# Plain columns of a split-precision matmul kernel: 96 wide in two matmuls per k, or 128 wide in three

## The chip, the cores and the metric

The kernel runs on one core of a Trainium2 chip. The metric is the device time of one execution in microseconds, the median of several runs. The profile comes from one execution, recorded by the hardware profiler.

## What is computed

Eight sequences of 256 tokens with 1024 features go through an adapter matrix chosen by an id for each sequence, then through a base layer with a routed low-rank (LoRA) part, and are added to the input:

```python
y      = einsum('bsi,boi->bso', x, weight[ids])            # stage 1, 1024 x 1024 per sequence
base   = einsum('btd,od->bto', y, base_W) + base_b         # stage 2
logits = einsum('btd,nd->btn', y, router_W) + router_b     # 15 router outputs
probs  = softmax(logits); topk_p, topk_i = top_k(probs, 8)
w      = einsum('btk,btke->bte', topk_p, onehot(expert_map[topk_i]))
h      = einsum('btd,erd->bter', y, A)                     # 8 experts x rank 16
out    = x + base + einsum('bter,eor->bto', h * w[..., None], B) * 2.0
```

## The kernel before

Everything is float32. Each operand of a matmul is split into a high part in the float32r format and a low part (value minus high part), and a product a x b is three matmuls: hi x hi, hi x lo, lo x hi. ScalarE writes the high parts (copies with a cast), VectorE the low parts (subtractions). Each matmul is preceded by its own load of 128 x 128 weights.

An **element** is one of the eight sequences (b). It has two stages on TensorE.

Stage 1 (`stage1_chunk`, L825 and L827) makes y in eight chunks of 128 outputs, eight steps of k each: one matmul of 512 columns (w_hi against x_hi and x_lo side by side) and one of 256 (w_lo against x_hi). ScalarE and VectorE add the two halves into y_sum and split it into y_hi and y_lo, and form differences of blocks of y (`sums`, `sums_lo`, `fourth`).

Stage 2 multiplies y by base_W, the router and A. Its 1024 output columns are divided in three: N1 and N2, NH = (1024 - NP)/2 wide, and PLAIN, NP wide between them. N1 and N2 are done by a block scheme with 7 instead of 8 half products (`product`, L860 to L862: 4 steps of k, three matmuls of NH columns each; 7 calls an element, 8 plain calls in element 0). The block combinations of base_W are in `st_hi` and `st_lo`. The three widths hang together: NP = 96 gives NH = 464.

The plain part (`plain`, L850 and L851) holds what is multiplied by the ordinary rule: AR = 8 x 16 + 15 + 1 = 144 columns for A, the router and one column of padding, and the NP plain columns of base_W; PL = AR + NP = 240. `pl_split[:, k, 0, :]` is the high part, `pl_split[:, k, 1, :]` the low part, and they lie side by side. For each of two token tiles t and eight k, L850 multiplies y_hi by both (2 x PL = 480 columns) and L851 adds y_lo times the high part to the first 240 columns. The product y_hi x lo thus stands in a second half of columns of `pl_ps`, and other engines add the halves: for the routing, ScalarE copies the second half (`ar_part`, L411) and VectorE adds the first (L581, in `routing_logits`); for the plain output columns, VectorE adds both halves to res in two instructions (`add_plain`, L641 and L643).

The order on TensorE in stage 2 of an element (`stage2`): plain, product into x_ps, into z_ps (from the differences S1), into x_ps (S2), the transposes of the gated h (L881), product into w_ps, x_ps, z_ps, three groups of three LoRA matmuls of 512 columns (`lora_b`, L875 to L877), one more product and one more LoRA group. Between them stand waits for the other engines by semaphores: s_lo_done (VectorE L557) before the z_ps product, hw_done (the end of the routing chain, L618) before the transposes, s4_lo_done (L570) before the last z_ps product, hwt_lo_done (L625) before the LoRA matmuls, x_added and z_added (VectorE's additions into res, L633 and L636) before the reuse of their tiles. Element 0 has its own order (`first_stage2`), in which the blocks of base_W are still being split (L699). Elements 1 to 6 run in a loop, element 7 stands behind it. SyncE issues nearly all transfers, GpSimd those with addition.

Of the kernel before, what the change touches and what calls it, by code (L numbers as in the profile page):

```python
# [12 lines left out]
ALU = mybir.AluOpType  # L13
# [23 lines left out]
def adaln_ffn_kernel(nc, xT, x, ids, wT, a_t, base_t, b_t, router_t, base_b, router_b, expert_map, out):  # L37
    NB, _, KC, T = xT.shape
    OC = wT.shape[1]
    D = KC * P  # L40
    NT = T // P
# [4 lines left out]
    AR = ER + NR + 1  # L46
    KH = KC // 2

    NP = 96
    NH = (D - NP) // 2  # L50
    PL = AR + NP
    DH = D // 2
    HALF = NP // 2
    N1, PLAIN, N2 = slice(0, NH), slice(NH, NH + NP), slice(NH + NP, D)
    H1, H2 = slice(0, DH), slice(DH, D)
    AT1, AT2 = slice(0, NH), slice(HALF, DH)
    assert 2 * PL <= 512 and DH <= 512 and OC == 2 * KH and NT == 2 and NB >= 4


    ORDER = [o for j in range(KH) for o in (j, j + KH)]  # L60
# [5 lines left out]
    with ExitStack() as ctx:  # L66
        def sem(name):
            return ctx.enter_context(nc.semaphore(name))
# [3 lines left out]
        def sb(name, shape, dt=F32, over=None):  # L72

            size = 4
            for n in shape[1:]:
                size *= n
            offset = spot[0] if over is None else over
            if over is None:
                spot[0] += (size + 31) // 32 * 32
                assert spot[0] <= SBUF_TO, (name, spot[0])  # L80
            return nc.alloc_sbuf_tensor_at(name, shape, dt, offset=offset)
# [18 lines left out]
        pl_split = sb("pl_split", [P, KC, 2, PL], F32R)  # L100
# [19 lines left out]
        res = sb("res", [P, NT, D])  # L120
# [29 lines left out]
        ar_sum = sb("ar_sum", [P, NT, AR])  # L150

        def bank(name, shape):
            return ctx.enter_context(nc.psum_tensor(name, shape, F32))

        y_ps = bank("y_ps", [P, 2, 512])
        pl_ps = bank("pl_ps", [P, NT, 512])
# [62 lines left out]
        s4_hi_done = sem("s4_hi_done")  # L219
        s4_lo_done = sem("s4_lo_done")  # L220
        ar_done = sem("ar_done")
        ar_part_done = sem("ar_part_done")
        ar_sum_done = sem("ar_sum_done")
        p1_done = sem("p1_done")
        p1_added = sem("p1_added")
        shifted = sem("shifted")
# [10 lines left out]
        z_added = sem("z_added")  # L237
        w_added = sem("w_added")
        v_added = sem("v_added")
        pl_part_added = sem("pl_part_added")  # L240
        pl_added = sem("pl_added")
        res_biased = sem("res_biased")
        chain_done = sem("chain_done")
# [140 lines left out]
        def _(act):  # L384
            def evacuate(b, c):
                act.wait_ge(y_ps_done, OC * b + c + 1)
                nc.scalar.copy(y_sum[:, ORDER[c], :], y_ps[:, c % 2, T:2 * T]).then_inc(y_part_done, 1)  # L387

            def make_y_hi(b, j):
                act.wait_ge(y_sum_done, OC * b + 2 * j + 2)  # L390
                nc.scalar.copy(y_hi[:, pair(j), :], y_sum[:, pair(j), :]).then_inc(y_hi_done, 1)  # L391

            def adapter_hi(b, c):
                act.wait_ge(w_in[c % W_SLOTS], 16 * w_uses(b, c))
                nc.scalar.copy(w_hi[:, c % W_SLOTS, :, :], w_raw[:, c % W_SLOTS, :, :]).then_inc(w_hi_done, 1)  # L395
# [8 lines left out]
            def sums_hi(b):  # L404

                act.wait_ge(s_done, KH * b)
                nc.scalar.copy(s_hi[:, :, :, :], s_ps[:, :, :].rearrange("p s (j t) -> p s j t", t=P)).then_inc(s_hi_done, 1)

            def ar_part(b):
                act.wait_ge(ar_done, 2 * b + 2)  # L410
                nc.scalar.copy(ar_sum[:, :, :], pl_ps[:, :, PL:PL + AR]).then_inc(ar_part_done, 1)  # L411

            def make_x_hi(b):
                for h in range(2):
                    k = slice(h * KH, (h + 1) * KH)
                    act.wait_ge(x_in[h], 16 * b)
                    nc.scalar.copy(x_split[:, k, 0, :], x_raw[:, k, 1, :]).then_inc(x_hi_done, 1)
# [5 lines left out]
            def exponential(b):  # L423
                act.wait_ge(shifted, b + 1)
                nc.scalar.activation(prob[:, :, :], shift[:, :, :], ACT.Exp).then_inc(exp_done, 1)

            def make_hwt_hi(b):
                act.wait_ge(hwt_done, b + 1)
                nc.scalar.copy(hwt_hi[:, :, :], v_ps[:, 0:T].rearrange("p (t n) -> p t n", n=P)).then_inc(hwt_hi_done, 1)
# [14 lines left out]
            def element(b, last=False):  # L444
                for c in range(OC):
                    if not last or c + 2 < OC:
                        adapter_hi(b, c + 2)
                    evacuate(b, c)
                    if c % 2:
                        make_y_hi(b, c // 2)  # L450
                    if isinstance(b, int) and b == 1 and c == 6:
                        act.wait_ge(t4_in, 16)
                        nc.scalar.copy(st_hi[:, :, T4, :], st_raw[:, :, T4, :]).then_inc(t4_hi_done, 1)
                sums_hi(b)
                if isinstance(b, int) and b == 1:
                    act.wait_ge(t3_in, 16)
                    nc.scalar.copy(st_hi[:, :, T3, :], st_raw[:, :, T3, :]).then_inc(t3_hi_done, 1)
                ar_part(b)
                exponential(b)
                if not last:  # L460
                    make_x_hi(b + 1)
                make_hwt_hi(b)
                fourth_hi(b)

            act.dma_start(x0_raw[:, :, :], xT[0]).then_inc(x0_in, 16)
            for j in range(PIECES):
                k = slice(j * KP, (j + 1) * KP)
# [3 lines left out]
            for j in range(PIECES):  # L471
                k = slice(j * KP, (j + 1) * KP)
# [19 lines left out]
                    block_hi(B00, hi_raw[:, :, T4, :])  # L492
            act.wait_ge(r10_in, 16)
            block_hi(B10, st_raw[:, :, T4, :])
            ar_part(0)
            act.wait_ge(t1_done, 1)
            nc.scalar.copy(st_hi[:, :, T1, :], st_raw[:, :, T2, :]).then_inc(t1_hi_done, 1)
            act.wait_ge(r11_in, 16)
# [13 lines left out]
            with act.Fori(2, NB - 1) as b:  # L512
                element(b)
# [3 lines left out]
        def _(dve):  # L517
# [57 lines left out]
            def routing_logits(b):  # L575
                at = 11 * b
                if isinstance(b, int) and b == 0:
                    dve.wait_ge(mask_done, 1 + E)
                    dve.wait_ge(small_in, 32)
                dve.wait_ge(ar_part_done, b + 1)  # L580
                nc.vector.tensor_tensor(ar_sum[:, :, :], pl_ps[:, :, 0:AR], ar_sum[:, :, :], ALU.add).then_inc(ar_sum_done, 1)  # L581
                dve.wait_ge(ar_sum_done, b + 1)
                nc.vector.tensor_tensor(logits[:, :, :], ar_sum[:, :, ER:ER + NR], per_tile(router_bias[:, :], NR),
                                        ALU.add).then_inc(chain_done, 1)
                dve.wait_ge(chain_done, at + 1)
                nc.vector.tensor_reduce(row_max[:, :], logits[:, :, :], AX.X, ALU.max).then_inc(chain_done, 1)
                for t in range(NT):
                    nc.vector.max(top8[:, t, :], logits[:, t, :]).then_inc(chain_done, 1)
                dve.wait_ge(chain_done, at + 4)
                nc.vector.tensor_tensor(shift[:, :, :], logits[:, :, :],  # L590
                                        row_max[:, :].rearrange("p (t n) -> p t n", n=1).to_broadcast([P, NT, NR]),
                                        ALU.subtract).then_inc(shifted, 1)
                for t in range(NT):
                    nc.vector.match_replace(marked[:, t, :], top8[:, t, :], logits[:, t, :], MARK).then_inc(chain_done, 1)
# [43 lines left out]
            def add_plain(b):  # L638

                dve.wait_ge(ar_done, 2 * b + 2)  # L640
                nc.vector.tensor_tensor(res[:, :, PLAIN], pl_ps[:, :, AR:PL], res[:, :, PLAIN], ALU.add).then_inc(pl_part_added, 1)  # L641
                dve.wait_ge(pl_part_added, b + 1)
                nc.vector.tensor_tensor(res[:, :, PLAIN], pl_ps[:, :, PL + AR:2 * PL], res[:, :, PLAIN], ALU.add).then_inc(pl_added, 1)  # L643

            def stage2(b, last):
                second = isinstance(b, int) and b == 1
# [103 lines left out]
            for j in range(PIECES):  # L750
                k = slice(j * KP, (j + 1) * KP)
                dve.wait_ge(x0_hi_done, j + 1)
                nc.vector.tensor_tensor(x_split[:, k, 1, :], x0_raw[:, k, :], x_split[:, k, 0, :], ALU.subtract).then_inc(x0_lo_done, 1)
            for j in range(PIECES):
                k = slice(j * KP, (j + 1) * KP)
# [59 lines left out]
        def _(pe):  # L815
# [25 lines left out]
            def plain(b, first=False):  # L841

                for t, part in ((1, 0), (0, 0), (1, 1), (0, 1)):
                    for k in PLAIN_ORDER[:KC - 2] if part == 0 else PLAIN_ORDER[KC - 2:]:
                        if first and t == 1 and k in (0, KH):
                            pe.wait_ge(pl_lo_done, k // KH + 1)
                        if t == 1 and k < KH:
                            pe.wait_ge(y_lo_done, KH * b + k + 1)
                        hi, lo = (y[:, k, t * P:(t + 1) * P] for y in (y_hi, y_lo))
                        nc.tensor.matmul(pl_ps[:, t, 0:2 * PL], hi, pl_split[:, k, :, :].rearrange("p s n -> p (s n)"), start=(k == 0), stop=False)  # L850
                        mm = nc.tensor.matmul(pl_ps[:, t, 0:PL], lo, pl_split[:, k, 0, :], start=False, stop=(k == KC - 1))  # L851
                    if part:
                        mm.then_inc(ar_done, 1)
# [175 lines left out]
```

## Time and profile before

| | us |
|---|---|
| median of 3 runs | 401.98 |
| lowest and highest run | 401.46, 401.98 |
| the profiled execution | 400.99 |
| its span, first to last instruction | 399.2 |
| TensorE matmul busy | 394.5 |
| VectorE busy | 301.5 |
| ScalarE busy | 159.0 |
| mean granted TensorE clock | 1.000 of full speed |

PE is the matmul engine TensorE, PEld its weight loads, DVE VectorE, ACT ScalarE, POOL GpSimd. Matmuls are pipelined: a matmul's row begins when it starts and ends when its last result is there, so neighbouring rows overlap. The time that one costs in a stream is the distance between its start and the next one's. Start times are in microseconds from the beginning of the span.

### The profile page before, as it was taken

The page shows a single profiled execution, that of the slowest core. Times are in us where ns is not written, and L with a number is a line of the kernel's source. Part 1 is how long each engine was busy: PE and PEld are TensorE (multiplying, and loading weights), DVE is VectorE, ACT ScalarE, POOL GpSimd, SP SyncE. Part 2 cuts the span into 40 slices and gives each one's busy share as a digit, 9 for nine tenths or more (in the row PEclk, how much of TensorE's full clock was granted, in tenths as well). Part 3 has the DMA queues.
Part 4 walks back from the last instruction along what each step waited for, and adds up shares of the span by engine and source line. Part 5 has one row for each costly group of instructions (what it writes and reads, how often), then busy time and mean ns, then how long its engine had stood idle before and what let it go on. Part 6 is the DMA issues. An engine that isn't in the chain of part 4 may idle for free.

```text
span 399.2 us, 5973 instructions
## 1 busy us (share of the span) xinstructions
PE 394.5 (99%) x2102; PEld 348.8 (87%) x2102; DVE 301.5 (76%) x554; ACT 159.0 (40%) x226; POOL 8.4 (2%) x22
## 2 busy tenths in 40 slices
PE   8999999999999999999999999999999999999996
PEld 8889888888888988888888888888888898888985
DVE  3868998798978874888658996589846898468763
ACT  4666434672156402553026530455304542144300
POOL 0002210000000000000000000000000000000000
PEclk9999999999999999999999999999999999999999
DMA  8999498730456306652076511774036830464002
GB/s 311 397 392 397 87 206 285 274 107 0 186 184 261 105 0 216 216 210 94 0 263 238 195 41 37 257 278 163 0 93 226 312 105 0 146 223 158 2 0 105
DMA packets 27133, 67.56 MB, mean 169 GB/s; under 512 B 3442, under 2 KB 14194, under 8 KB 26994
## 3 DMA queue, kind: packets, MB, share of 16 engines
q1 hardware_dynamic: 25106, 62.47, 43.6%
q0 software_dynamic: 1872, 3.90, 4.9%
q10 hardware_dynamic: 144, 1.05, 0.7%
q8 instruction: 6, 0.10, 0.1%
q14 instruction: 5, 0.04, 0.0%
HBM read 58.08 MB, written 8.39 MB: 167 GB/s over the span
## 4 chain that ended last, share of the span: by engine, by line
PE 99%; DVE 0%; POOL 0%; issue 0%; POOLq 0%
PE y_ps L825 29%; PE y_ps L827 15%; PE pl_ps L850 7%; PE x_ps L861 6%; PE x_ps L860 6%; PE x_ps L862 6%; PE s_ps L861 6%; PE s_ps L862 6%; PE s_ps L860 6%; PE pl_ps L851 4%; PE s_ps L951 1%; PE s_ps L875 1%; PE s_ps L877 1%; PE s_ps L876 1%; PE y_ps L838 1%; PE x_ps L877 0%
## 5 line engine op out<-in xcount | busy, mean ns | idle before, releaser
L825 PE MATMUL y_ps<-x_split,w_hi 128*128 128x512 f32 x504 | 176.1, 393 | 0.0
L827 PE MATMUL y_ps<-x_split,w_lo 128*128 128x256 f32 x504 | 141.2, 280 | 0.0
L825 PEld LDWEIGHTS y_ps<-x_split,w_hi 128*128 128x128 f32 x504 | 94.4, 187 | 21.4
L827 PEld LDWEIGHTS y_ps<-x_split,w_lo 128*128 128x128 f32 x504 | 95.2, 189 | 0.3
L395 ACT CAST w_hi<-w_raw 128x1024 fp32r<-128x1024 f32 x58 | 60.8, 1050 | 69.5 <-DMA w_raw<-in_wT 69.1
L521 DVE TENSOR_TENSOR w_lo<-w_raw,w_hi 128x1024 fp32r<-128x1024 f32 x58 | 70.8, 1224 | 13.0 <-ACT w_hi L395 11.3
L387 ACT COPY y_sum<-y_ps 128x256 f32<-128x256 f32 x63 | 23.5, 373 | 67.1 <-PE y_ps L827 67.1
L850 PE MATMUL pl_ps<-pl_split,y_hi 128*128 128x480 f32 x128 | 42.7, 383 | 0.0
L539 DVE TENSOR_TENSOR y_sum<-y_ps,y_sum 128x256 f32<-128x256 f32 x63 | 26.6, 422 | 20.5 <-ACT y_sum L387 20.2
L851 PE MATMUL pl_ps<-pl_split,y_lo 128*128 128x240 f32 x128 | 34.9, 273 | 0.0
L860 PE MATMUL s_ps<-st_hi,y_hi 128*128 128x464 f32 x80 | 30.4, 380 | 0.0
L861 PE MATMUL s_ps<-st_lo,y_hi 128*128 128x464 f32 x80 | 29.9, 373 | 0.0
L633 DVE TENSOR_TENSOR res<-s_ps,res 128x512 f32<-128x512 f32 (+1 forms) x31 | 20.3, 678 | 12.5 <-PE s_ps L877 12.4
L862 PE MATMUL s_ps<-st_hi,y_lo 128*128 128x464 f32 x80 | 29.7, 372 | 0.0
L391 ACT CAST y_hi<-y_sum 128x512 fp32r<-128x512 f32 x32 | 19.9, 622 | 19.2 <-DVE y_sum L539 19.2
L850 PEld LDWEIGHTS pl_ps<-pl_split,y_hi 128*128 128x128 f32 x128 | 24.0, 188 | 4.0
L543 DVE TENSOR_TENSOR y_lo<-y_sum,y_hi 128x512 fp32r<-128x512 f32 x32 | 22.2, 693 | 5.5 <-ACT y_hi L391 2.7
L633 DVE TENSOR_TENSOR res<-x_ps,res 128x512 f32<-128x512 f32 (+1 forms) x15 | 10.0, 668 | 18.9 <-PE x_ps L877 15.4
L851 PEld LDWEIGHTS pl_ps<-pl_split,y_lo 128*128 128x128 f32 x128 | 24.3, 190 | 0.0
L861 PE MATMUL x_ps<-st_lo,y_hi 128*128 128x464 f32 x64 | 23.9, 373 | 0.0
L860 PE MATMUL x_ps<-st_hi,y_hi 128*128 128x464 f32 x64 | 23.8, 373 | 0.0
L862 PE MATMUL x_ps<-st_hi,y_lo 128*128 128x464 f32 x64 | 23.8, 371 | 0.0
(114 smaller groups left out, 542.1 us busy)
## 6 DMA issues: line engine op xcount, KB each, us to landing
w_raw<-in_wT SPq DMA_DIRECT2D x60, 512.0 KB, 3.3
res<-in_x SPq DMA_DIRECT2D x16, 512.0 KB, 4.2
x_raw<-in_xT SPq DMA_DIRECT2D x14, 512.0 KB, 4.7
out<-res SPq DMA_DIRECT2D x13, 512.0 KB, 3.0
early_raw<-in_wT SPq DMA_DIRECT2D x4, 512.0 KB, 7.8
hi_raw<-in_base_t SPq DMA_DIRECT2D x2, 928.0 KB, 9.9
st_raw<-in_base_t SPq DMA_DIRECT2D x2, 928.0 KB, 11.5
st_raw<-in_base_t POOLq DMA_DIRECT2D x2, 928.0 KB, 9.6
```

Of the source, the lines that this page charges most:

```text
L387: nc.scalar.copy(y_sum[:, ORDER[c], :], y_ps[:, c % 2, T:2 * T]).then_inc(y_part_done, 1)
L395: nc.scalar.copy(w_hi[:, c % W_SLOTS, :, :], w_raw[:, c % W_SLOTS, :, :]).then_inc(w_hi_done, 1)
L521: nc.vector.tensor_tensor(w_lo[:, s, :, :], w_raw[:, s, :, :], w_hi[:, s, :, :], ALU.subtract).then_inc(w_lo_done, 1)
L539: nc.vector.tensor_tensor(y_sum[:, o, :], y_ps[:, c % 2, 0:T], y_sum[:, o, :], ALU.add).then_inc(y_sum_done, 1)
L633: return nc.vector.tensor_tensor(res[:, t, cols], ps, res[:, t, cols], ALU.add)
L825: nc.tensor.matmul(y_ps[:, c % 2, :], w_hi[:, s, k, :], x_split[:, k, :, :].rearrange("p s t -> p (s t)"), start=(k == 0), stop=False)
L827: mm = nc.tensor.matmul(y_ps[:, c % 2, 0:T], w_lo[:, s, k, :], x_split[:, k, 0, :], start=False, stop=(k == KC - 1))
L850: nc.tensor.matmul(pl_ps[:, t, 0:2 * PL], hi, pl_split[:, k, :, :].rearrange("p s n -> p (s n)"), start=(k == 0), stop=False)
L851: mm = nc.tensor.matmul(pl_ps[:, t, 0:PL], lo, pl_split[:, k, 0, :], start=False, stop=(k == KC - 1))
L860: nc.tensor.matmul(dst, hi(j), st_hi[:, j, block_of, :], start=begins and j == 0, stop=False, skip_group_check=not begins)
L861: nc.tensor.matmul(dst, hi(j), st_lo[:, j, block_of, :], start=False, stop=False, skip_group_check=not begins)
L862: mm = nc.tensor.matmul(dst, lo(j), st_hi[:, j, block_of, :], start=False, stop=(j == KH - 1), skip_group_check=not begins)
```

## The change

NP becomes 2 x (512 - 448) = 128, so NH is 448, and PL is 272. Two times 272 columns don't fit one bank of 512, and the plain part is now three matmuls of 272 columns per tile and k, all into the same 272 columns. The second half of columns is gone, and with it VectorE's addition for the routing (ScalarE's copy now takes the first 144 columns, and the logits are made from it) and one of the two additions of the plain output.

```diff
-    NP = 96
+    NP = 2 * (D // 2 - 448)
     NH = (D - NP) // 2
     PL = AR + NP
...
-    assert 2 * PL <= 512 and DH <= 512 and OC == 2 * KH and NT == 2 and NB >= 4
+    assert PL <= 512 and DH <= 512 and OC == 2 * KH and NT == 2 and NB >= 4
...
-            def ar_part(b):
+            def ar_copy(b):
                 act.wait_ge(ar_done, 2 * b + 2)
-                nc.scalar.copy(ar_sum[:, :, :], pl_ps[:, :, PL:PL + AR]).then_inc(ar_part_done, 1)
+                nc.scalar.copy(ar_sum[:, :, :], pl_ps[:, :, 0:AR]).then_inc(ar_copy_done, 1)
...
-                dve.wait_ge(ar_part_done, b + 1)
-                nc.vector.tensor_tensor(ar_sum[:, :, :], pl_ps[:, :, 0:AR], ar_sum[:, :, :], ALU.add).then_inc(ar_sum_done, 1)
-                dve.wait_ge(ar_sum_done, b + 1)
+                dve.wait_ge(ar_copy_done, b + 1)
                 nc.vector.tensor_tensor(logits[:, :, :], ar_sum[:, :, ER:ER + NR], per_tile(router_bias[:, :], NR),
                                         ALU.add).then_inc(chain_done, 1)
...
-                nc.vector.tensor_tensor(res[:, :, PLAIN], pl_ps[:, :, AR:PL], res[:, :, PLAIN], ALU.add).then_inc(pl_part_added, 1)
-                dve.wait_ge(pl_part_added, b + 1)
-                nc.vector.tensor_tensor(res[:, :, PLAIN], pl_ps[:, :, PL + AR:2 * PL], res[:, :, PLAIN], ALU.add).then_inc(pl_added, 1)
+                nc.vector.tensor_tensor(res[:, :, PLAIN], pl_ps[:, :, AR:PL], res[:, :, PLAIN], ALU.add).then_inc(pl_added, 1)
...
-                        nc.tensor.matmul(pl_ps[:, t, 0:2 * PL], hi, pl_split[:, k, :, :].rearrange("p s n -> p (s n)"), start=(k == 0), stop=False)
+                        nc.tensor.matmul(pl_ps[:, t, 0:PL], hi, pl_split[:, k, 0, :], start=(k == 0), stop=False)
+                        nc.tensor.matmul(pl_ps[:, t, 0:PL], hi, pl_split[:, k, 1, :], start=False, stop=False)
                         mm = nc.tensor.matmul(pl_ps[:, t, 0:PL], lo, pl_split[:, k, 0, :], start=False, stop=(k == KC - 1))
```

## Rows read from the trace of the kernel before

**Rows 1.** The page, busy times by engine and granted clock in 40 slices.
```profile
PE 394.5 (99%) x2102; PEld 348.8 (87%) x2102; DVE 301.5 (76%) x554; ACT 159.0 (40%) x226; POOL 8.4 (2%) x22
PEclk9999999999999999999999999999999999999999
```
**Rows 2.** The page, the chain that ended last, by engine and by line.
```profile
PE 99%; DVE 0%; POOL 0%; issue 0%; POOLq 0%
PE y_ps L825 29%; PE y_ps L827 15%; PE pl_ps L850 7%; PE x_ps L861 6%; PE x_ps L860 6%; PE x_ps L862 6%; PE s_ps L861 6%; PE s_ps L862 6%; PE s_ps L860 6%; PE pl_ps L851 4%; PE s_ps L951 1%; PE s_ps L875 1%; PE s_ps L877 1%; PE s_ps L876 1%; PE y_ps L838 1%; PE x_ps L877 0%
```
**Rows 3.** TensorE's waits: who for whom, total us, times, longest.
```profile
PE s_ps L951 <- POOL ident L967: 1.5, 1, 1.5
```
**Rows 4.** The page, groups of instructions: the plain part (busy us, mean ns, idle before).
```profile
L850 PE MATMUL pl_ps<-pl_split,y_hi 128*128 128x480 f32 x128 | 42.7, 383 | 0.0
L851 PE MATMUL pl_ps<-pl_split,y_lo 128*128 128x240 f32 x128 | 34.9, 273 | 0.0
```
**Rows 5.** Timeline, TensorE, elements 1 and 2, plain part: start us, duration, instruction.
```profile
81.30 0.38 PE L850 MATMUL pl_ps<-pl_split,y_hi 128*128 128x480 f32 x1
...
129.41 0.38 PE L850 MATMUL pl_ps<-pl_split,y_hi 128*128 128x480 f32 x1
...
129.95 0.27 PE L851 MATMUL pl_ps<-pl_split,y_lo 128*128 128x240 f32 x1
130.06 0.38 PE L850 MATMUL pl_ps<-pl_split,y_hi 128*128 128x480 f32 x1
...
134.69 0.37 PE L860 MATMUL x_ps<-st_hi,y_hi 128*128 128x464 f32 x1
```
**Rows 6.** Timeline, TensorE, element 2, the rest of stage 2.
```profile
142.25 0.38 PE L881 MATMUL s_ps<-ident,hw 128*128 128x128 f32 x2
...
147.52 0.37 PE L860 MATMUL s_ps<-st_hi,y_hi 128*128 128x464 f32 x1
...
150.04 0.40 PE L875 MATMUL s_ps<-b_split,hwt_hi 128*128 128x512 f32 x1
...
152.10 0.38 PE L860 MATMUL x_ps<-st_hi,y_hi 128*128 128x464 f32 x1
```
**Rows 7.** Timeline, TensorE, starts of stage 1 in elements 1 and 2.
```profile
58.70 0.39 PE L825 MATMUL y_ps<-x_split,w_hi 128*128 128x512 f32 x1
...
107.22 0.39 PE L825 MATMUL y_ps<-x_split,w_hi 128*128 128x512 f32 x1
107.45 0.28 PE L827 MATMUL y_ps<-x_split,w_lo 128*128 128x256 f32 x1
```
**Rows 8.** Timeline, weight loads of the plain part.
```profile
129.63 0.19 PEld L850 LDWEIGHTS pl_ps<-pl_split,y_hi 128*128 128x128 f32 x1
129.73 0.19 PEld L851 LDWEIGHTS pl_ps<-pl_split,y_lo 128*128 128x128 f32 x1
```
**Rows 9.** The warm-up's line: ns min/median/max, first and last start.
```profile
L951 PEld LDWEIGHTS s_ps<-ident x26: 263/333/333, 1.5 to 6.8; 128*128 128x128 f32 x26
```
**Rows 10.** Groups of instructions: VectorE's additions of the column halves.
```profile
L581 DVE TENSOR_TENSOR ar_sum<-pl_ps,ar_sum 128x288 f32<-128x288 f32 x8 | 3.6, 456 | 1.7 <-ACT ar_sum L411 1.7
L643 DVE TENSOR_TENSOR res<-pl_ps,res 128x192 f32<-128x192 f32 x8 | 2.9, 358 | 0.3
```
**Rows 11.** Timeline, VectorE, element 2: what TensorE waits for.
```profile
133.30 1.75 DVE L557 TENSOR_TENSOR s_lo<-s_ps,s_hi 128x1536 fp32r<-128x1536 f32 x1
...
139.66 0.43 DVE L618 TENSOR_TENSOR hw<-ar_sum,gate_n 128x256 f32<-128x256 f32 x1
...
143.59 0.69 DVE L570 TENSOR_TENSOR y_lo<-y_sum,y_hi 128x512 fp32r<-128x512 f32 x1
```
**Rows 12.** Timeline, element 0: VectorE's first block, TensorE's first product.
```profile
32.65 2.08 DVE L699 TENSOR_TENSOR st_lo<-hi_raw,st_hi 128x1856 fp32r<-128x1856 f32 x1
...
35.59 0.37 PE L860 MATMUL s_ps<-st_hi,y_hi 128*128 128x464 f32 x1
```

More of the change, by code:

```diff
@@ L221, in adaln_ffn_kernel @@
         ar_done = sem("ar_done")
-        ar_part_done = sem("ar_part_done")
-        ar_sum_done = sem("ar_sum_done")
+        ar_copy_done = sem("ar_copy_done")
         p1_done = sem("p1_done")
@@ L239, in adaln_ffn_kernel @@
         v_added = sem("v_added")
-        pl_part_added = sem("pl_part_added")
         pl_added = sem("pl_added")
@@ L457, in element @@
                     nc.scalar.copy(st_hi[:, :, T3, :], st_raw[:, :, T3, :]).then_inc(t3_hi_done, 1)
-                ar_part(b)
+                ar_copy(b)
                 exponential(b)
@@ L494, in _ @@
             block_hi(B10, st_raw[:, :, T4, :])
-            ar_part(0)
+            ar_copy(0)
             act.wait_ge(t1_done, 1)
```

## The prediction

> **What bounds the kernel now.** I read the page's first part, then the chain of work that ended last, then the waits of TensorE, and only then single start times. The matmul engine is busy 394.5 of 399.2 us and no other engine is over 76% [rows 1]. The chain consists of TensorE's own lines, 99% of the span, with the stage 1 lines L825 and L827 at 44% [rows 2]. TensorE waits for another engine once, 1.5 us, before its very first instruction [rows 3]. The granted clock is full (9 in each of the 40 slices, 1.000 as the mean of the profiled run), which is the higher level, 2.4 GHz [rows 1]. So the kernel's time is a sum over TensorE's instructions, and a change is worth what it changes in the time from one matmul's start to the next one's. The mean durations of the groups (383 ns for 480 columns, 273 for 240 [rows 4]) can't be used for this, because neighbouring matmuls overlap; I use differences of start times, and over long stretches, since the rows are rounded to 10 ns.
>
> **Start to start, by width.** The plain part of element 2 begins at 129.41 and the products at 134.69: 5.28 us for 16 steps of k, 330 ns for a 480 and a 240 together, of which 110 is the 240 (129.95 to 130.06) and so 220 the 480 [rows 5]. The 36 products of 464 columns from 134.69 to the transposes at 142.25 take 210.0 ns each; nine matmuls of 512 from 150.04 to 152.10 take 228.9 each [rows 5, 6]. In stage 1, 64 pairs of 512 and 256 take from 107.22 to 129.41: 346.7 a pair, of which 230 is the 512, so 116.7 the 256 [rows 5, 7]. What is over the columns at 2.4 per ns is 10 ns for 240 and for 256, 16.7 for 464, 20 for 480 and 15.6 for 512. It grows with width, though not evenly.
>
> **The plain part.** Per tile and k, 480 + 240 columns become three times PL = 144 + 128 = 272. No row has 272. From 256 at 116.7 I add 16 columns at 0.43 ns (between 0.42, from 240 to 256, and 0.44, from 256 to 512) and get 123.6, taken as 124. Low end: 0.39 a column, the slope from 464 to 512, gives 122.9. High end: 113.3 for the columns and the 480's surplus of 20, 133. I take 124 since 272 lies beside 256 and far from 480. A step goes from 330 to 372, +42; there are 2 tiles x 8 k x 8 elements = 128 steps, the count of L850 [rows 4]: **+5.4 us**, ends +5.0 (3 x 122.9) and +9.0 (3 x 133.3).
>
> **The products.** 464 columns become 448. Their number is 12 instructions x (8 products in element 0 + 7 in each of 7 others) = 684. At the same 0.43 they lose 6.9 each, 203.1 ns: **-4.7 us**. Ends: the slope from 464 to 512 gives -6.3 each, -4.3 us; the slope from 464 to 480, which is 10 ns for 16 columns, gives 200 ns each and -6.8 us. I take 0.43 because it spans the wide gap from 256 to 512 and also holds from 240 to 256; the step from 464 to 480 rests on two widths that stand in different lines.
>
> **The same, counted in columns.** Element 0: +1,536 plain, -1,536 products. Each of the other seven: +1,536 and -1,344. Together +1,344 columns, 0.56 us at 2.4 per ns. The widths therefore nearly cancel by themselves, and the sum is decided by the surplus per instruction, of which there are 128 more. Stage 1, the lora matmuls and the transposes are unchanged.
>
> The Trainium skill, page "TensorE: Matmul & The Clock Gate", section "Back-to-back issue gap", has N / 2.4 + 2.5 ns for a lone stream of matmuls. By that rule a step would go from 305 to 347.5 and a product lose 6.7, +5.4 and -4.6, together +0.9 us. The trace disagrees with its level, 228.9 ns against 215.8 for 512 columns [rows 6], and hardly with its slope.
>
> **Weight loads.** Before, 128 x 2; after, 128 x 3, one before each matmul. Two consecutive matmuls take the same y_hi block now. I give no saving for that, as L860 and L861 share their weights too and each has a load of its own: there are 2102 loads for 2102 matmuls [rows 1]. A load's row is 0.19 us long, but loads overlap: two start at 129.63 and 129.73, some 100 ns apart [rows 8]. The 240-wide matmul therefore covers the next load in 110 ns at present, and a 272-wide one has 124. I cost the loads at nothing, covered by the matmul before. What no row shows is three short matmuls in a row at full clock: now each short one follows a long one. The nearest is the warm-up: 26 records of 128-wide passes between 1.5 and 6.8, 213 ns apart, under loads whose rows are 333 long [rows 9]. There loads overlap one after another, at a spacing of 0.64 of a row's length; 124 over 190 is 0.65. It is just enough, and so a rival remains.
>
> The same page of the Trainium skill, section "Measured speedup vs the span model", says that a weight load overlaps a running matmul only where its row group differs. By that rule and the 107 ns that the page's section "LDWEIGHTS (loading the stationary operand)" gives for 128 columns, each added matmul would cost 107 more, an estimate of 13.7 us for 128. The trace disagrees: all these loads use all 128 rows and still lie under matmuls only 110 apart [rows 5, 8].
>
> **The other engines.** VectorE loses L581 (456 ns) and one of L641 and L643 (about 350) per element; the remaining plain add has 256 elements for 192, some 70 ns more [rows 10]. ScalarE's copy keeps its size. None of it is on the chain, so it is worth 0. What counts is that no wait becomes late. The routing result is ready when L618 ends, 139.66 + 0.43 = 140.09, while the transposes start at 142.25: 2.2 us in hand [rows 6, 11]. After, the 36 products before it take 0.25 less, but L581's 0.46 leaves the same chain, so the slack grows. s_lo ends at 135.05 for the second product, which starts 12 x 0.21 after 134.69, at 137.21, and moves 0.7 later with the plain part; the fourth block's lo ends at 144.28 for the product at 147.52 [rows 5, 6, 11]. Element 0 is tighter: its first st_lo ends at 34.73, its first product starts at 35.59 [rows 12]. There the plain part moves the deadline 16 x 42 = 0.67 later, so the 0.86 in hand grows. The setup loads change size slightly (928 to 896 KB per block, 192 to 256 KB per half of the plain columns) and TensorE waits for none of them; cost 0; if that cover were gone, each us by which a block comes later costs a us, once. The tail after the last matmul, an add of 512 columns and its store, is untouched.
>
> **Sum.** 399.2 + 5.4 - 4.7 = 399.9 us of span. With the 1.8 us around it, the profiled execution of 400.99 becomes 401.7. That execution is 1.0 below the median of the runs, 401.98; on the median the sum gives **402.7**. The outer ends of the two terms are -1.8 and +4.7.
>
> **Rivals.**
> (a) The surplus steps up between 256 and 272 columns, to 16 or 20 ns as for 464 and 480. For: there is no width between 256 and 464 in the trace, and the surplus does differ. Against: it does not move from 240 to 256. 129.3 to 133.3 ns give +7.4 to +9.0 for the plain part, net +2.7 to +4.3: 404.7 to 406.3.
> (b) Weight loads or issue bound the run of short matmuls. Place: the 48 consecutive 272s of each element. It decides once a load-and-matmul pair can't follow at 124 ns. The mean spacing is 165 now in the plain part and 173 in stage 1, so nothing proves a sustained 124. At 140 the step is 420, +11.5 less 4.7: +6.8, 408.8; it could be far more.
> (c) It ends faster: the products gain more than their columns. Mechanism: the surplus of a product falls to 13 ns at 448 (200 ns each, the step that separates 480 from 464), while 272 stays at 123. Then -6.8 + 5.0 = -1.8: 400.2. It decides as soon as the products save over 5.4 / 684 = 7.9 ns each, that is 448 columns under 202.1. For: 464 and 480 are 10 ns apart. Against: 464 and 512 are 19 apart for 48 columns.
> (d) The change doesn't do what it says, or the repeated weights aren't loaded: the time differs by less than can be told from 401.98, or the gain is hidden anyway.
>
> **How the numbers follow.** The forecast (+0.0 to +1.6 net) has 0.48, (a) 0.14, (b) 0.10, (c) with all of -1.8 to -0.1 has 0.20, (d) 0.08. A difference under 0.2%, 0.8 us, is about what a measurement of this kernel can't tell from none. The forecast splits into 0.30 under that and 0.18 over it; (c) into 0.14 faster and 0.06 same; (d) is same; (a) and (b) are slower. So faster 0.14, same 0.44, slower 0.42. The range leaves out (b), the top of (a) and the last bit of (c): 400.4 to 405.8.
>
> **What would show each step.** First starts of the plain part and of the products: 5.95 us for the 48 matmuls of an element where 5.28 stood, and 7.31 for 36 products where 7.56 stood. Alternate 272s at 124 and 140 or a rise of the loads' rows above 190 would speak for (b); even 129 to 133 for (a); products at 200 for (c). TensorE's list of waits should still have its one entry. The prediction is wrong if a new wait stands in that list, or if stage 1, which holds 44% of the chain, changes its 346.7 per pair. That could happen, since the 64 pairs of element 1 take 22.60 us (58.70 to 81.30) against 22.19 in element 2 [rows 5, 7], for no reason that I can read off.

## The result and the profile after

The changed kernel takes 404.60 us, the median of four runs (404.26 to 405.67), against 401.75 for the kernel before (four runs): a ratio of 1.0076, 95% interval 1.0061 to 1.009. In a second series on another occasion it was 403.85 against 401.34, ratio 1.0058, interval 1.0045 to 1.007. So it is slower by 2.5 to 2.9 us. It lies within the predicted range of 400.4 to 405.8, but 1.9 us over the predicted 402.7.

The page of the changed kernel, first the busy times and the granted clock, then the chain that ended last, and TensorE's groups in stage 1 and the plain part:

```profile
PE 397.0 (98%) x2230; PEld 357.7 (89%) x2230; DVE 294.3 (73%) x538; ACT 158.6 (39%) x226; POOL 10.0 (2%) x22
PEclk9999999999999999999999999999999999999999
PE 95%; DMA 3%; DVE 1%; ACT 0%; SPq 0%; issue 0%
L819 PE MATMUL y_ps<-x_split,w_hi 128*128 128x512 f32 x504 | 178.1, 398 | 0.6 <-DVE y_sum L537 0.6
L821 PE MATMUL y_ps<-x_split,w_lo 128*128 128x256 f32 x504 | 141.3, 280 | 0.0
L844 PE MATMUL pl_ps<-pl_split,y_hi 128*128 128x272 f32 x128 | 37.0, 289 | 0.0
L844 PEld LDWEIGHTS pl_ps<-pl_split,y_hi 128*128 128x128 f32 x128 | 24.1, 188 | 0.4
```

L819 and L821 are stage 1 (L825 and L827 before), L844 to L846 the plain part, L855 to L857 the products. The 128 added matmuls with their loads are there (2230 for the 2102 of [rows 1]), at full clock, and the loads' rows are as long as before.

The profiled run of the changed kernel was the slowest of its four, at 405.67. TensorE's waits (total us, times, longest) show two that the kernel before does not have, the first and the third line here; the second is that of [rows 3]:

```profile
PE y_ps L832 <- DMA w_raw<-in_wT: 1.6, 1, 1.6
PE s_ps L946 <- POOL ident L962: 1.5, 1, 1.5
PE y_ps L819 <- DVE y_sum L537: 0.6, 1, 0.6
```

Both stand behind a transfer of adapter weights, one at the start, one at 79 us. The chain's 3% DMA are mostly these two transfers, 4.9 and 6.1 us long; what they added to the time is far less. The second series (e1 below) had the first wait at 0.2 us and the second not at all, with a span of 402.7. I therefore count with that profile: 402.7 against 399.2, +3.5 us of span. That is 1.0 more than the 2.5 between the medians of the second series, because the two profiled executions lie on either side of their medians: 400.99 for 401.34 before, 404.55 for 403.85 after.

Start times of TensorE in element 2 of the changed kernel (start us, duration, instruction): stage 1, plain part, products, transposes, and stage 1 of element 3.

```profile
108.62 0.39 PE L819 MATMUL y_ps<-x_split,w_hi 128*128 128x512 f32 x1
...
131.22 0.29 PE L844 MATMUL pl_ps<-pl_split,y_hi 128*128 128x272 f32 x1
131.35 0.29 PE L845 MATMUL pl_ps<-pl_split,y_hi 128*128 128x272 f32 x1
131.47 0.29 PE L846 MATMUL pl_ps<-pl_split,y_lo 128*128 128x272 f32 x1
131.59 0.29 PE L844 MATMUL pl_ps<-pl_split,y_hi 128*128 128x272 f32 x1
...
137.24 0.36 PE L855 MATMUL x_ps<-st_hi,y_hi 128*128 128x448 f32 x1
...
144.54 0.38 PE L876 MATMUL s_ps<-ident,hw 128*128 128x128 f32 x2
...
157.41 0.39 PE L819 MATMUL y_ps<-x_split,w_hi 128*128 128x512 f32 x1
```

The plain part takes 137.24 - 131.22 = 6.02 us for 48 matmuls, 125.4 ns each (single distances lie between 122 and 130), where 5.28 stood [rows 5]. The 36 products take 7.30, 202.8 each, where 7.56 stood [rows 5, 6]. Both are near the forecast (5.95 and 7.31). What is not: stage 1 takes 131.22 - 108.62 = 22.60 us, 353.1 ns a pair, where the same 64 pairs took 129.41 - 107.22 = 22.19, 346.7 [rows 5, 7]. Not one of TensorE's instructions in stage 1 was changed, nor the addresses that they read and write, nor their widths. The kernel before shows 22.60 once too, in element 1 (81.30 - 58.70) [rows 5, 7]. The group's mean gives it away in one number: 398 ns for the 512-wide matmul in the changed kernel, 393 in the kernel before:

```profile
L825 PE MATMUL y_ps<-x_split,w_hi 128*128 128x512 f32 x504 | 176.1, 393 | 0.0
```

From start times like these in e1's profile the +3.5 us of span come out as: plain part 8 x 0.74 = +5.9; everything behind it in stage 2 8 x 0.63 = -5.0 (20.00 for 20.63 in element 2, the same within 0.02 in the others); stage 1 6 x 0.41 = +2.5 in elements 2 to 7, -0.2 in element 1 (22.39 for 22.60), nothing in element 0; the start +0.4 to +0.5 (the first of these pairs begins at 10.79 for 10.34).

### The profile page after: what moved, and what is told of

It reads as the page before. It is cut to its first block, busy times and chain, and to the rows that moved or that the text cites. A ratio compares the mean times of both kernels' runs of the same rounds, so it can differ in the third digit from the quotient of the medians.

```text
span 403.9 us, 6213 instructions
## 1 busy us (share of the span) xinstructions
PE 397.0 (98%) x2230; PEld 357.7 (89%) x2230; DVE 294.3 (73%) x538; ACT 158.6 (39%) x226; POOL 10.0 (2%) x22
## 4 chain that ended last, share of the span: by engine, by line
PE 95%; DMA 3%; DVE 1%; ACT 0%; SPq 0%; issue 0%
PE y_ps L819 28%; PE y_ps L821 14%; PE x_ps L857 6%; PE x_ps L855 6%; PE x_ps L856 6%; PE s_ps L855 5%; PE s_ps L857 5%; PE s_ps L856 5%; PE pl_ps L844 4%; PE pl_ps L846 4%; PE pl_ps L845 4%; DMA w_raw<-in_wT 3%; PE s_ps L871 1%; PE s_ps L872 1%; PE s_ps L870 1%; PE y_ps L832 1%
## 5 line engine op out<-in xcount | busy, mean ns | idle before, releaser
L819 PE MATMUL y_ps<-x_split,w_hi 128*128 128x512 f32 x504 | 178.1, 398 | 0.6 <-DVE y_sum L537 0.6
L821 PE MATMUL y_ps<-x_split,w_lo 128*128 128x256 f32 x504 | 141.3, 280 | 0.0
L819 PEld LDWEIGHTS y_ps<-x_split,w_hi 128*128 128x128 f32 x504 | 94.7, 188 | 24.1 <-DVE w_lo L519 0.9
L821 PEld LDWEIGHTS y_ps<-x_split,w_lo 128*128 128x128 f32 x504 | 95.1, 189 | 0.3
L844 PE MATMUL pl_ps<-pl_split,y_hi 128*128 128x272 f32 x128 | 37.0, 289 | 0.0
L846 PE MATMUL pl_ps<-pl_split,y_lo 128*128 128x272 f32 x128 | 36.9, 288 | 0.0
L845 PE MATMUL pl_ps<-pl_split,y_hi 128*128 128x272 f32 x128 | 36.7, 287 | 0.0
L855 PE MATMUL s_ps<-st_hi,y_hi 128*128 128x448 f32 x80 | 29.9, 374 | 0.0
L857 PE MATMUL s_ps<-st_hi,y_lo 128*128 128x448 f32 x80 | 29.2, 365 | 0.0
L856 PE MATMUL s_ps<-st_lo,y_hi 128*128 128x448 f32 x80 | 29.2, 365 | 0.0
L844 PEld LDWEIGHTS pl_ps<-pl_split,y_hi 128*128 128x128 f32 x128 | 24.1, 188 | 0.4
L845 PEld LDWEIGHTS pl_ps<-pl_split,y_hi 128*128 128x128 f32 x128 | 24.4, 190 | 0.0
L846 PEld LDWEIGHTS pl_ps<-pl_split,y_lo 128*128 128x128 f32 x128 | 24.1, 188 | 0.0
L855 PE MATMUL x_ps<-st_hi,y_hi 128*128 128x448 f32 x64 | 23.4, 366 | 0.0
```

The source lines that it names most:

```text
L819: nc.tensor.matmul(y_ps[:, c % 2, :], w_hi[:, s, k, :], x_split[:, k, :, :].rearrange("p s t -> p (s t)"), start=(k == 0), stop=False)
L821: mm = nc.tensor.matmul(y_ps[:, c % 2, 0:T], w_lo[:, s, k, :], x_split[:, k, 0, :], start=False, stop=(k == KC - 1))
L844: nc.tensor.matmul(pl_ps[:, t, 0:PL], hi, pl_split[:, k, 0, :], start=(k == 0), stop=False)
L845: nc.tensor.matmul(pl_ps[:, t, 0:PL], hi, pl_split[:, k, 1, :], start=False, stop=False)
L855: nc.tensor.matmul(dst, hi(j), st_hi[:, j, block_of, :], start=begins and j == 0, stop=False, skip_group_check=not begins)
L856: nc.tensor.matmul(dst, hi(j), st_lo[:, j, block_of, :], start=False, stop=False, skip_group_check=not begins)
```

## The experiments

Two cadences of stage 1 recur below: a **fast** one with 22.19 us for 64 pairs, in which every 512 from the third pair on takes 230 ns, and a **slow** one with 22.60, in which three pairs repeat (232, 241 and 236 for the 512s). The question was what picks the one or the other.

**The changed kernel once more** (no edit).

> The changed kernel once more, without an edit, for a second profile. Theory: its 2.9 us over the kernel before are +6.0 (48 matmuls of 272 an element at 125.5 ns), -4.9 (products at 203), and about +2 from stage 1, whose pairs of 512 and 256 columns take 353.3 ns in elements 2 to 7 where they took 346.7. In this second profile the same three terms stand, while the 1.6 us wait for the first weights and the 1.1 us stall at 78 us, both behind a transfer, are chance and may be missing: a span near 402.5. Rival: the stall at 78 us belongs to the change and stands here again.

403.85 us against 401.34, span 402.7. Stage 1 of elements 2 to 7 takes 22.60 us again in each, element 1 22.39. The stall at 79 us is gone, and none of the later profiles has it: it was chance. The three terms stood. Element 1 began fast and changed over in the middle:

```profile
59.28 0.39 PE L819 MATMUL y_ps<-x_split,w_hi 128*128 128x512 f32 x1
...
69.73 0.42 DVE L537 TENSOR_TENSOR y_sum<-y_ps,y_sum 128x256 f32<-128x256 f32 x1
...
70.38 0.39 PE L819 MATMUL y_ps<-x_split,w_hi 128*128 128x512 f32 x1
...
81.67 0.29 PE L844 MATMUL pl_ps<-pl_split,y_hi 128*128 128x272 f32 x1
```

The first four chunks, to 70.38, take 2.77 to 2.78 us each, the fast cadence; the last four take 2.81 to 2.83, the slow one. The change falls on a border between chunks, where TensorE asks for VectorE's sums (`y_sum_done`), and the last of these had ended 0.23 us earlier (70.15). The first profile changed over at the same border.

**The form alone**: 96 plain columns, three matmuls of 240.

```diff
-    NP = 2 * (D // 2 - 448)
+    NP = 96
```

> The form alone: 96 plain columns and products of 464 as before, but the plain part as three matmuls of 240 into the same columns. Theory: a step of k takes 3 x 111 to 112 = 333 to 336 ns against 330, +0.4 to +0.8 us in all, and stage 1 is at either 346.7 or 353.3 a pair, depending on how it is entered (up to +2.6 us more for six elements). Rival A, the three-matmul form itself slows stage 1: 353.3 in all loop elements, 404.5 or more. Rival B, it is the widths that slow it: 346.7 and 402.3.

402.04 us, ratio 1.0016 (1.0006 to 1.0026). Starts of stage 1, the plain part and the products in element 2:

```profile
107.47 0.39 PE L819 MATMUL y_ps<-x_split,w_hi 128*128 128x512 f32 x1
...
129.66 0.27 PE L844 MATMUL pl_ps<-pl_split,y_hi 128*128 128x240 f32 x1
...
135.04 0.37 PE L855 MATMUL x_ps<-st_hi,y_hi 128*128 128x464 f32 x1
```

The plain part takes 5.38 us, 112.1 ns for each 240, against 5.28 before: 0.10 x 8 = +0.8 us for the form. Stage 1 is fast (22.19) in elements 2 to 7 and slow in element 1, as in the kernel before. So the form doesn't slow stage 1, and costs 0.8 us at most: the added 128 weight loads are covered.

**112 plain columns in the old form.**

```diff
-    NP = 96
+    NP = 112
```

> A width between, in the old form: 112 plain columns, PL 256, two matmuls of 512 and 256 a step, products of 456 columns. By stage 1's own rows a step takes 347 to 353, +2.1 to +3.0 us, and 684 products save 3.5 each, -2.4 us: -0.3 to +0.6 us against before. With the slow cadence in six elements of stage 1 2.6 us come on top, if the entry decides it; if the three-matmul form or the width 448 is the cause, stage 1 stays at 346.7.

401.32 us, ratio 1.0000 (0.9991 to 1.0009). Products of 456 and plain matmuls of 512 and 256 columns cancel to within the measurement. Stage 1 is fast in elements 2 to 7 and slow in element 1, as in the kernel before. An unchanged repeat was made to see if that is chance:

> 112 plain columns in the old form once more, unchanged, for a second look at which elements are slow. In its first profile element 1 had the plain step at 358.8 and stage 1 at 353.3, the others 346.6 and 346.7. Theory: the cadences are the same again, element by element, as they follow from the instruction stream. Rival: they vary by chance from run to run.

It gave 401.6 us and again 22.60 us in element 1 and 22.19 in element 2; the plain steps of element 1 were at 353 instead of 359 ns. The cadence of elements 1 to 7 was the same in both profiles, as it is if it follows from the instruction stream. That of element 0 was not: its seven chunks took 19.6 us in one profile and 19.9 in the other.

**A delay ahead of stage 1**: one useless matmul, of 64 columns, in elements 1 to 7 of the changed kernel.

```diff
+                if c == 0 and not (isinstance(b, int) and b == 0):
+                    nc.tensor.matmul(y_ps[:, 0, 0:64], w_hi[:, 0, 0, :], x_split[:, 0, 0, 0:64], start=True, stop=True)
                 for k in range(KC):
```

> The changed kernel with one useless matmul of 64 columns ahead of stage 1 in elements 1 to 7. It costs 30 to 40 ns seven times, +0.3 us. Theory (the cadence is chosen by the moment at which stage 1 begins within the stream): the pairs of elements 2 to 7 leave 353.3, and if they fall into 346.7 the time is 404.6 + 0.3 - 2.6 = 402.3; at the least some element's cadence differs from that without it. Rival (the cadence is a property of the layout or of the other engines' work): 353.3 everywhere, 404.9.

405.27 us, and stage 1 is slow in all seven elements, so the hoped-for 402.3 was missed. But it is not without effect: element 1, which begins fast in both profiles of the changed kernel, is now slow from its first pairs on. The next kernel has the loop written out and widths of 128 + 16 b in its place.

> The changed kernel with TensorE's loop written out and one useless matmul ahead of stage 1 in elements 1 to 7, of 144, 160, 176, 192, 208, 224 and 240 columns. With 64 columns it was bound by its weight load and the cadence stayed 353.3. Each costs 60 to 110 ns, about +0.6 us. Theory (entry): the seven different delays give both cadences, some elements at 346.7 and some at 353.3. Rival: all at 353.3.

A miss as well: 405.05 us in its one run, all seven elements slow. Element 7, with the 240-wide one:

```profile
351.09 0.27 PE L817 MATMUL y_ps<-x_split,w_hi 128*128 128x240 f32 x1
...
373.81 0.29 PE L846 MATMUL pl_ps<-pl_split,y_hi 128*128 128x272 f32 x1
```

22.72 us with the useless matmul, 0.12 over 22.60; with 64 and with 160 columns it was 22.72 too. From the start of the useless matmul to that of the first 256-wide one it is 341 to 345 ns for every width, so the eight widths are hardly different delays: they don't rule out that the moment at which stage 1 begins decides.

**The two widths parted**: three plain matmuls of 272, 32 of the columns zero padding, and products of 464.

```diff
-    NP = 2 * (D // 2 - 448)
+    NP = 96
     NH = (D - NP) // 2
-    PL = AR + NP
+    PL = AR + NP + 32
...
-                nc.vector.tensor_tensor(res[:, :, PLAIN], pl_ps[:, :, AR:PL], res[:, :, PLAIN], ALU.add).then_inc(pl_added, 1)
+                nc.vector.tensor_tensor(res[:, :, PLAIN], pl_ps[:, :, AR:AR + NP], res[:, :, PLAIN], ALU.add).then_inc(pl_added, 1)
...
```

> Three matmuls of 272 columns a step as in the changed kernel, but only 96 of the 128 plain columns are used (32 of the 272 are zero padding) and the products are 464 wide as before. This parts the two widths of the change. Plain step 376 ns as in the changed kernel (+5.9 us against before), products 210 as before. If the products' width, which runs right before stage 1, decides stage 1's cadence: 346.7 from element 2 on, and 401.4 + 5.9 = 407.3. If the 272-wide plain part decides it: 353.3, and 2.5 more, 409.8.

406.98 us against 401.15, ratio 1.0139. Element 2:

```profile
108.60 0.39 PE L819 MATMUL y_ps<-x_split,w_hi 128*128 128x512 f32 x1
...
130.79 0.29 PE L844 MATMUL pl_ps<-pl_split,y_hi 128*128 128x272 f32 x1
...
136.82 0.37 PE L855 MATMUL x_ps<-st_hi,y_hi 128*128 128x464 f32 x1
```

The plain part costs its 6.03 us, and stage 1 is fast, 22.19, in elements 2 to 7 (slow in element 1). The instruction sequence on TensorE is that of the changed kernel, only the products' width differs, and with it the addresses of the tiles that lie behind `st_hi`: with 464 fast, with 448 slow. The 272-wide plain part is cleared.

**The last two groups of an element exchanged**, in the changed kernel: the same instructions in another order.

```diff
-                product(x_ps, y_block(1, 1), T4, begins=False)
-                lora_b(1, x_ps, H1).then_inc(x_ps_done, 1)
+                lora_b(1, x_ps, H1)
+                product(x_ps, y_block(1, 1), T4, begins=False).then_inc(x_ps_done, 1)
```

> The changed kernel with the last product and the last LoRA group of each element (1 to 7) in the other order: same instructions, no work added, but stage 1 is entered from 448-wide matmuls and not from 512-wide ones. Theory (the entry chooses the cadence): the pattern of start distances at the entry changes and may fall into 346.7 a pair; six or seven elements of stage 1 then save 0.41 us each, 403.9 - 2.5 = 401.4. If it stays in 353.3, the time stays 403.9 and the order isn't what chooses. Rival (the layout or the other engines' work sets it): 353.3, 403.9.

401.67 us against 401.15, ratio 1.0009 (0.9998 to 1.0021), where the unexchanged one has 1.0058. Groups, then the start of the plain part and what stands on either side of stage 1 in element 2:

```profile
L819 PE MATMUL y_ps<-x_split,w_hi 128*128 128x512 f32 x504 | 175.3, 391 | 0.0
106.37 0.37 PE L857 MATMUL x_ps<-st_hi,y_lo 128*128 128x448 f32 x1
106.58 0.39 PE L819 MATMUL y_ps<-x_split,w_hi 128*128 128x512 f32 x1
...
128.77 0.29 PE L844 MATMUL pl_ps<-pl_split,y_hi 128*128 128x272 f32 x1
...
134.79 0.36 PE L855 MATMUL x_ps<-st_hi,y_hi 128*128 128x448 f32 x1
```

All of elements 1 to 7 are fast now (22.19), the plain part is still 6.02, and the span is 399.1. Elements 2 to 7 are the exchange's doing. Element 1 is not: it stands behind element 0, whose order was left alone, and began fast without the exchange too; here it stayed fast to its end, and at the border where it changed over in e1 VectorE's sum had ended 0.38 us earlier, not 0.23.

**The same exchange in the kernel before.**

> The same exchange in the kernel before, where elements 2 to 7 run at 346.7: theory, the entry from 464-wide matmuls may throw them into 353.3 (up to +2.5 us, 403.9) or pull element 1 into 346.7 (-0.4). Rival: no pair changes, 401.4.

403.76 us, ratio 1.0061 (1.0045 to 1.0076): the kernel before becomes as slow as the changed one, by nothing but the order of two groups. Its group and element 2:

```profile
L825 PE MATMUL y_ps<-x_split,w_hi 128*128 128x512 f32 x504 | 178.1, 398 | 0.0
106.91 0.37 PE L862 MATMUL x_ps<-st_hi,y_lo 128*128 128x464 f32 x1
107.12 0.39 PE L825 MATMUL y_ps<-x_split,w_hi 128*128 128x512 f32 x1
...
129.72 0.38 PE L850 MATMUL pl_ps<-pl_split,y_hi 128*128 128x480 f32 x1
```

22.60 us in each of elements 1 to 7; element 1, again not behind an exchange, was so before.

**The exchange in element 3 alone**, loop written out, in the changed kernel.

```diff
+                if isinstance(b, int) and b == 3:
+                    lora_b(1, x_ps, H1)
+                    product(x_ps, y_block(1, 1), T4, begins=False).then_inc(x_ps_done, 1)
+                else:
```

> The changed kernel with TensorE's loop written out and the exchange of the last product and the last LoRA group in element 3 alone. Theory: what stands right before stage 1 chooses its cadence, each time anew: element 4's stage 1 takes 346.7 a pair (22.19 us), elements 2, 3, 5, 6 and 7 take 353.3 (22.60). Rival: the stream keeps a state from element to element, so that elements 4 to 7 all change; or it is the loop's place in the program, and none changes.

403.8 us in one run, which can't show the 0.4 us expected; the trace can. Stage 1 and the start of the plain part in elements 3, 4 and 5:

```profile
155.97 0.39 PE L819 MATMUL y_ps<-x_split,w_hi 128*128 128x512 f32 x1
...
178.57 0.29 PE L844 MATMUL pl_ps<-pl_split,y_hi 128*128 128x272 f32 x1
...
204.55 0.39 PE L819 MATMUL y_ps<-x_split,w_hi 128*128 128x512 f32 x1
...
226.74 0.29 PE L844 MATMUL pl_ps<-pl_split,y_hi 128*128 128x272 f32 x1
...
252.77 0.39 PE L819 MATMUL y_ps<-x_split,w_hi 128*128 128x512 f32 x1
...
275.37 0.29 PE L844 MATMUL pl_ps<-pl_split,y_hi 128*128 128x272 f32 x1
```

22.60, 22.19, 22.60: the one element behind the exchange is fast and the next is slow again. In this profile the choice is made anew at each entry, by what stands before it, and the slow cadence needs no loop. (Element 1, not shown, kept the fast pattern and took 22.33 us, 0.14 of them in a delay at 70 us.)

**Toward a faster version**: the exchange at the end of element 0 only, in the kernel before, whose element 1 is slow.

```diff
-                product(v_ps, y_block(1, 1), B11, begins=False, at=AT2)
-                lora_b(1, v_ps, H2).then_inc(v_ps_done, 1)
+                lora_b(1, v_ps, H2)
+                product(v_ps, y_block(1, 1), B11, begins=False, at=AT2).then_inc(v_ps_done, 1)
```

> The kernel before with the last product and the last LoRA group of element 0 exchanged, as element 1 is the one that runs at 353.3 there. Theory: element 1's stage 1 leaves that cadence, and its 22.60 us become 22.19: 401.2 - 0.4 = 400.8. The others keep 346.7. If element 1 stays at 353.3, the time stays.

Element 1 becomes fast and the others stay so; the span is 398.5:

```profile
58.45 0.40 PE L825 MATMUL y_ps<-x_split,w_hi 128*128 128x512 f32 x1
...
80.63 0.38 PE L850 MATMUL pl_ps<-pl_split,y_hi 128*128 128x480 f32 x1
```

That is 22.18 us. The times, 400.99 against 401.18, ratio 1.0000 (0.9988 to 1.0011), can't tell it from the kernel before. The same with 112 plain columns:

> 112 plain columns in the old form, with the exchange at the end of element 0. Theory: element 1's stage 1 goes from 22.60 to 22.19 us, and its plain step perhaps from 358.8 to 346.7 with it (0.2 us): 401.3 - 0.4 to 0.6 = 400.7 to 400.9, below the kernel before by 0.1%, at the edge of what can be told.

401.19 us, ratio 1.0003 (0.9991 to 1.0016). Stage 1 of element 1 is fast (59.20 to 81.38), but its plain part took 6.80 us, 1.0 of them in a wait:

```profile
PE pl_ps L850 <- DVE y_lo L543: 1.0, 1, 1.0
```

I can't say from one profile whether that wait belongs to the version. No version was found that is measurably faster than the kernel before.

## Why the prediction was right or wrong

The forecast sum was +0.7 us and 2.5 to 2.9 were measured. The 404.60 lies within the range by luck: the room above 402.7 was made for dearer plain matmuls (rival (a), 404.7 to 406.3), and what filled it was stage 1, which has no term in the range.

**The bound** was read rightly: TensorE's own stream sets the time, and it moved only by what the stream costs.

**The plain part** was forecast at 372 ns a step and +5.4 us. It is 376 and +5.9: 272 columns cost 125.4 ns, not 124. Rival (a) called for 129 to 133 and is out; the surplus over the columns is 12 ns, close to the 10 of 256.

**The products** were forecast at 203.1 and are 202.8; -4.7 us against -4.9 measured. Rival (c) needed less than 202.1 together with 123 for the 272 and is out.

**The weight loads** were costed at nothing. Three 240s in a row take 112.1 ns each (e2), against 330 / 3 = 110 before: rival (b) is out, and the whole form costs 0.8 us. What I called just enough was enough. The rule that the prediction quotes, that a load overlaps a running matmul only where its row group differs, stands in the section "The mechanism" of the Trainium skill's page "TensorE: Matmul & The Clock Gate", not in the one it names; e2's 0.8 us, against the 13.7 estimated by it, contradicts it once more.

**The other engines** were costed at nothing, and rightly: the changed kernel has no listed wait of TensorE within its elements that stands in both profiles.

The sum of these was +0.7 and is +1.0. e6 shows the change with stage 1 fast, at a ratio of 1.0009, +0.4 to +0.5 us: that is about the case that I had priced, and 0.4 us better in element 1, which is slow in the kernel before.

**The step that failed** is the sentence "Stage 1, the lora matmuls and the transposes are unchanged". Their instructions are; the time of stage 1 is not. It rose by 0.41 us in six elements, +2.5, less 0.2 in element 1: about three times what I had forecast in all. The prediction had seen that element 1 took 22.60 and element 2 22.19 and named a change of the 346.7 as what would make it wrong, but gave it neither a price nor a chance. By that sign of its own it was wrong here. It should have been a rival with both: up to six elements x 0.41 us to the slow side, and 0.4 for element 1 to the fast side. The trace had the two levels ready.

That the order of the last groups picks the cadence is shown: the exchange flipped it in e6, e7, e9 and e10, with every width and address as it was. That the products' width does so is nearly shown: e5 differs from the changed kernel on TensorE in that width alone, but some tiles also lie at other addresses. Why is open. A state kept over elements doesn't explain it (e9). The moment of the start is not ruled out, since e4 and e8 tried in effect one delay, and it did change element 1. I have no view of what happens within the engine.

## What to carry to other kernels

When a stream of matmuls is the bound, measure its cadence from start to start in every repetition of a stage, not only in one: two levels for the same instructions are a term of the sum, even where the change doesn't touch them. Trading columns between two parts of such a stream is worth what column count and per-instruction surplus say, here +1.0 us for 1,344 columns and 128 instructions more, and not the busy time of the engines relieved. And before a slowdown is put down to an edit, reorder something neutral next to the stage that got slower.

## What the runs showed of the hardware

The same 128 instructions of stage 1, at full clock and without a wait, run at 346.7 or 353.3 ns a pair, and in elements 2 to 7 keep to one of them from the third pair on, in all fourteen profiles. Exchanging 12 matmuls with 3 ahead of the stage was enough to flip it in either direction (a ratio of 1.0009 to the kernel before in place of 1.0058, and 1.0061 in place of 1).

In both profiles of the changed kernel, element 1 began fast and went over to slow at the border of its fifth chunk: hence the 22.39 us in the second. So the cadence can also be lost on the way. VectorE's sum had ended 0.21 and 0.23 us before that border, 0.38 in e6, where the cadence held; in e9, with 0.15, TensorE began the chunk 0.14 us late and the fast cadence held too. Whether the late sum is the cause is not shown.

One extra matmul with its own weight load, put ahead of stage 1, costs 0.12 us, whether it has 64, 160 or 240 columns (e4, e8), while 240-wide ones in a row cost 112.1 ns each (e2). Between 64 and 240 columns a narrower extra matmul saved nothing here.
